# Work shared out anew between VectorE and GpSimd, and reordered edges, in a two-layer fp32 kernel on one core

## The chip, the cores and the metric

The kernel runs on one core of a Trainium2 chip. The metric is the device time in microseconds (us); here the median over runs of the whole program. The engines are TensorE (PE, with its weight loads PEld), VectorE (DVE), ScalarE (ACT), GpSimd (POOL) and SyncE (SP), which issues most DMAs.

## The reference

```python
def lora_add(base, inp, A, B):          # A, B picked per batch by itok_B_2_6
    t = jnp.einsum('bri,bni->bnr', Ab, inp)
    return base + jnp.einsum('bor,bnr->bno', Bb, t) * SCALE
gate = lora_add(jnp.einsum('bnh,fh->bnf', x, W_gate), x, A_gate, B_gate)
up = lora_add(jnp.einsum('bnh,fh->bnf', x, W_up), x, A_up, B_up)
act = jax.nn.silu(gate) * up
x = x + lora_add(jnp.einsum('bnf,hf->bnh', act, W_down), act, A_down, B_down)
...
base = jnp.einsum('bsi,oi->bso', x, weight) + bias
low = jnp.einsum('bsi,bri->bsr', x, a_sel)
x = x + base + scale[:, None, None] * jnp.einsum('bsr,bor->bso', low, b_sel)
```

x is 8 batches of 256 tokens by 1024, the hidden layer has 2752 features, all in fp32.

## The kernel before

**Numbers in two parts.** Each fp32 operand is kept as a high part (rounded to fp32r) and a low part (the rest). ACT writes the high part, then DVE or POOL subtracts it from the original and writes the low part; PE multiplies high x high, high x low and low x high. So each weight tile and each part of x takes an ACT instruction (`w_high` L1355, `x_high` L1384, `b_high` L1439) and a low one behind it (on POOL `w_low` L1784, `x_low` L1788, `ag_low` L1793; on DVE `x_low` L605, `b_low` L638). All matmuls have line L1898.

**Phase A (gate and up, to about 935 us).** The tokens are taken in two halves `h`. Each half has 22 units: 21 of 128 features (unit `u` of gate and up together) and a half tile of 64. A unit is a 2x2 block product: rows are gate (A11, A12: its tile's two chunks along the inner dimension) and up (A21, A22), columns are two groups of tokens of x (B11, B21 and B12, B22). Units 0 and 1 are plain: eight products of 12 matmuls. From the third unit on a unit takes seven products, P1 = A11 x B11, P6 = S2 x T2, P5 = S1 x T1, P7 = S3 x T3, P2 = A12 x B21, P4 = A22 x T4, P3 = S4 x B22, in that order on PE. S1 to S4 are sums of weight tiles (DVE, L530 to L540), T1 to T4 sums of x parts (DVE, `x_sum` L601); each T comes in two chunks (`kq` 0 and 1). T3 takes the place of B12. Since the T's are needed first in the third unit, they are made while units 0 and 1 run, by `first_unit(U)` and `second_unit(U)`, which exist on every engine and are each engine's hand-written order of work. The half tile (last unit of a half) has P1, P2 and a stage C = N x T2 + S x B22. ACT copies P1 to `p1buf` (`copy_p1` L1392); DVE's `add_q` (L664) adds P6 to it, which frees the bank that P7 fills; `add_v` (L670) does so ahead of P4.

**The adapters.** x times A (tiles `AG`, turned by `turn_ag`) gives t in PSUM; DVE adds its two pieces and masks each (`t_sum` L647 and L650, eight instructions), ACT makes the high part and DVE the low part (`t_low` L656, four). `Bf` is the B side of a unit (`b_low(U)`, two instructions). PE's adapters of units 0 and 1 read `Tm_g`, `Tm_u` (t) and `Bf`. Weight tiles are turned by DVE (L504), after their load by SP.

**Phase B (down projection, 935 to 1460 us).** 11 blocks, each 16 (k, pr) steps; DVE adds each result to `acc` (L923, `add_down`). `D` items are the down weights (`Wd`). The last block also sums, masks (L906) and splits the adapter's `tw_down` into `Td` (`td_low` L941) for `pr` 0 and 1, and POOL makes `X1lo` (L1842) for phase C, the second layer.

**What orders the work.** Every engine runs its own hand-written list; waits are on semaphores that count along fixed lists (`Order`: `x_sums`, `x_lo_d` for low parts on DVE, `x_lo_p` on POOL). Weight parts go through a ring of four buffers W_58 to W_61. In names of instructions X_T_51 is T2, X_T_53 is T1, X_T_54 is T3, X_T_55 is T4, X_B_49, 50 and 52 are B11, B21 and B22; xs_62 and xs_63 are buffers for T1's and T2's sums, xt_56 and xt_57 hold turned x; s_74 to s_77 are S1 to S4.

## Time and profile before

| | us |
|---|---|
| median of 3 runs (1665.5 to 1667.55) | 1667.23 |
| the profiled execution | 1668.35 |
| its span | 1666.6 |
| PE busy | 1624.7 (97%) |
| PE weight loads | 1316.6 (79%) |
| DVE | 1130.3 (68%) |
| POOL | 662.3 (40%) |
| ACT | 501.2 (30%) |

Times in the rows are in us from the span's start, durations of groups and instructions too. A row of the timeline gives start, length, engine, line, operation, tiles, count of instructions merged, and in brackets the idle time ahead of it with what ended that. Busy shares are averages over very different stretches; what counts is which wait ends last at a given place.

### The profile page before, as it was taken

The page shows a single profiled execution, that of the slowest core. Times are in us where ns is not written, and L with a number is a line of the kernel's source. Part 1 is how long each engine was busy: PE and PEld are TensorE (multiplying, and loading weights), DVE is VectorE, ACT ScalarE, POOL GpSimd, SP SyncE. Part 2 cuts the span into 40 slices and gives each one's busy share as a digit, 9 for nine tenths or more (in the row PEclk, how much of TensorE's full clock was granted, in tenths as well). Part 3 has the DMA queues.
Part 4 walks back from the last instruction along what each step waited for, and adds up shares of the span by engine and source line. Part 5 has one row for each costly group of instructions (what it writes and reads, how often), then busy time and mean ns, then how long its engine had stood idle before and what let it go on. Part 6 is the DMA issues. An engine that isn't in the chain of part 4 may idle for free.

```text
span 1666.6 us, 20956 instructions
## 1 busy us (share of the span) xinstructions
PE 1624.7 (97%) x7060; PEld 1316.6 (79%) x7060; DVE 1130.3 (68%) x1298; ACT 501.2 (30%) x833; POOL 662.3 (40%) x445
## 2 busy tenths in 40 slices
PE   5999999999999999999999999999999999999998
PEld 4778888888877788888888788888888887778886
DVE  4987777777768877777777655666665578756433
ACT  3543333333345433333334221111111122431110
POOL 4254445444453554444444443233333331541110
PEclk9999999999999999999999999999999999999999
DMA  7344434423533434344334751222222131013322
GB/s 153 82 105 105 142 93 116 143 79 86 135 86 80 105 105 143 102 107 142 83 88 131 247 147 57 53 79 80 79 53 77 61 69 28 18 29 79 79 49 55
DMA packets 218127, 156.13 MB, mean 94 GB/s; under 512 B 110692, under 2 KB 200164, under 8 KB 215268
## 3 DMA queue, kind: packets, MB, share of 16 engines
q1 hardware_dynamic: 169792, 115.05, 27.4%
q10 hardware_dynamic: 48100, 39.73, 7.5%
...
q0 software_dynamic: 128, 0.00, 0.0%
...
## 4 chain that ended last, share of the span: by engine, by line
PE 64%; DVE 1%; POOL 1%; issue 1%; ACT 0%; ACTq 0%; DVEq 0%
PE ps L1898 64%; POOL act L1824 0%; DVE acc L923 0%; POOL Wd L1832 0%; DVE tw_down L906 0%; DVE Bd L869 0%; POOL W L1784 0%; DVE tw_down L897 0%; ACT W L1355 0%; DVE TU L504 0%; DVE ct L1039 0%; DVE turned L853 0%; DVE s L530 0%; DVE co L1061 0%; DVE c21buf L683 0%
## 5 line engine op out<-in xcount | busy, mean ns | idle before, releaser
L1898 PE MATMUL ps<-act,Wd 128*128 128x512 f32 x2016 | 462.6, 390 | 4.2 <-DVE acc L923 3.1
L1898 PE MATMUL ps<-X_T,W 128*128 128x512 f32 x1944 | 460.3, 391 | 6.4 <-POOL W L1784 1.8
L1898 PEld LDWEIGHTS ps<-act,Wd 128*128 128x128 f32 x2016 | 378.5, 188 | 84.9 <-DVE acc L923 3.6
L1898 PE MATMUL ps<-X_B,W 128*128 128x512 f32 x1728 | 423.2, 395 | 22.2 <-ACT X_B L1384 13.8
L1898 PEld LDWEIGHTS ps<-X_T,W 128*128 128x128 f32 x1944 | 363.0, 188 | 91.3 <-DVE vbuf L670 7.8
L1898 PEld LDWEIGHTS ps<-X_B,W 128*128 128x128 f32 x1728 | 328.4, 191 | 95.8 <-issue 22.7
L923 DVE TENSOR_TENSOR acc<-acc,ps 128x1024 f32<-128x1024 f32 x176 | 214.4, 1220 | 183.6 <-PE ps L1898 183.1
L1784 POOL TENSOR_TENSOR W<-s,W 128x512 fp32r<-128x512 f32 x156 | 211.8, 1358 | 236.5 <-ACT W L1355 236.5
L1784 POOL TENSOR_TENSOR W<-TG,W 128x512 fp32r<-128x512 f32 x88 | 129.8, 1476 | 148.9 <-ACT W L1355 148.8
L1355 ACT ACTIVATE W<-s 128x512 fp32r<-128x512 f32 x156 | 98.7, 632 | 280.4 <-PE ps L1898 272.1
L1824 POOL TENSOR_TENSOR act<-stage,act 128x1024 fp32r<-128x1024 f32 x42 | 100.5, 2410 | 175.4 <-ACT act L1574 175.4
L1898 PE MATMUL ps<-X1hi,Wo 128*128 128x512 f32 x512 | 141.4, 390 | 0.0
L1898 PEld LDWEIGHTS ps<-X1hi,Wo 128*128 128x128 f32 x512 | 96.1, 188 | 20.6
L1574 ACT ACTIVATE act<-stage 128x1024 fp32r<-128x1024 f32 x42 | 42.6, 1050 | 186.2 <-PE ps L1898 165.6
L664 DVE TENSOR_TENSOR qbuf<-p1buf,ps 128x512 f32<-128x512 f32 x38 | 26.1, 688 | 106.1 <-PE ps L1898 105.9
L1832 POOL TENSOR_TENSOR Wd<-turned,Wd 128x512 fp32r<-128x512 f32 x44 | 55.8, 1292 | 74.0 <-ACT Wd L1608 74.0
L1355 ACT ACTIVATE W<-TG 128x512 fp32r<-128x512 f32 x88 | 55.2, 628 | 91.1 <-PE ps L1898 90.7
L1784 POOL TENSOR_TENSOR W<-TU,W 128x512 fp32r<-128x512 f32 x46 | 63.6, 1385 | 45.8 <-ACT W L1355 45.8
L1898 PE MATMUL ps<-X1lo,Wo 128*128 128x512 f32 x256 | 80.3, 390 | 0.0
L1439 ACT ACTIVATE Bf<-ts 32x256 fp32r<-32x256 f32 (+1 forms) x176 | 71.9, 409 | 1.6
L1832 POOL TENSOR_TENSOR Wo<-turned,Wo 128x512 fp32r<-128x512 f32 x16 | 21.7, 1381 | 126.7 <-ACT Wo L1608 126.7
L686 DVE TENSOR_TENSOR c21buf<-c21buf,s1buf 128x512 f32<-128x512 f32 x38 | 68.7, 1808 | 1.3
...
## 6 DMA issues: line engine op xcount, KB each, us to landing
...
```

Source lines behind the costliest of these rows:

```text
L664: V.tensor_tensor(qbuf[:, :], p1buf[:, :], bank(U % 2, "b"), ALU.add).then_inc(q_done, 1)
L686: V.tensor_tensor(c21buf[:, :], c21buf[:, :], s1buf[:, :], ALU.mult).then_inc(act1_done, 1)
L923: V.tensor_tensor(acc[pr][:, k, :], acc[pr][:, k, :], src[:, :], ALU.add).then_inc(b_added.up(s), 1)
L1355: A.activation(hi, src, ACT.Copy).then_inc(w_hi, 1)
L1439: last = A.activation(home, src, ACT.Copy)
L1574: A.activation(acts[t % 3][:, 0, cols], stage[t % 2][:, cols], ACT.Copy).then_inc(act_hi.up((t, pr)), 1)
L1784: G.tensor_tensor(low, src, hi.bitcast(F32), ALU.subtract).then_inc(w_lo, 1)
L1824: G.tensor_tensor(acts[t % 3][:, 1, cols], stage[t % 2][:, cols], acts[t % 3][:, 0, cols].bitcast(F32), ALU.subtract).then_inc(act_lo.up(( ...
L1832: last = G.tensor_tensor(low, src, hi.bitcast(F32), ALU.subtract)
L1898: return nc.tensor.matmul(dst, stationary, moving, start=start, stop=stop, skip_group_check=True)
```

## The change

1. T2's sum always goes to xs_63 (before, its two chunks used both buffers). The order of sums becomes T1, T2, T1, T4, T2, T3, T3, T4; T4's first sum is made ahead of `t_sum` in the first unit.
2. The low parts of T2 (both chunks) and of T1's second go from DVE to POOL.
3. In the second unit DVE turns the third unit's tiles and makes S1, S2 ahead of T3, T4 and of the plain units' activations; ACT and POOL follow.
4. Half tile: PE does N x T2 between P1 and P2; in half 0's DVE makes B21's low part before it turns Ag. ACT and POOL write N ahead of A12.
5. The first down product waits for its low weight part four matmuls later.
6. Last block: masks leave `add_down` and become `td_mask`, pair 0 directly ahead of its low parts, pair 1 after the add (5, 0), low parts of pair 1 after (6, 0); ACT makes `Td`'s high part of pair 1 one X1hi later.
7. Eight DMAs of Ag(0, 0) are issued by ACT instead of SP.

```diff
@@ -138,7 +138,7 @@
                 return xs[0][:, :, :]
             if name == "T2":
-                return xs[1 - kq][:, :, :]
+                return xs[1][:, :, :]
...
@@ -203,7 +203,7 @@
             if u == FULL:
-                return ["P1", "P2", "C"]
+                return ["P1", "N", "P2", "C"]
...
@@ -301,16 +301,16 @@
                          [i for i in RAW_ORDER if i[0] in "xy" and i[:2] != ("x", 0)])
         x_sums = Order("x_sums", [(h, n, kq) for h in range(HALVES) for n, kq in (
-            ("T1", 0), ("T2", 0), ("T1", 1), ("T2", 1), ("T3", 0), ("T3", 1), ("T4", 0), ("T4", 1))])
...
         x_lo_d = Order("x_lo_d", [(h, n, kq) for h in range(HALVES) for n, kq in (
             *((("B11", 0), ("B21", 0), ("B12", 0)) if h == 0 else (("B12", 0), ("B11", 0), ("B21", 0))),
-            ("B11", 1), ("B12", 1), ("T1", 0), ("T2", 0), ("T1", 1), ("T2", 1), ("T4", 1), ("T3", 1))])
+            ("B11", 1), ("B12", 1), ("T1", 0), ("T3", 1), ("T4", 1))])
         x_lo_p = Order("x_lo_p", [(h, n, kq) for h in range(HALVES) for n, kq in (
-            ("B22", 0), ("B21", 1), ("B22", 1), ("T4", 0), ("T3", 0))])
+            ("B22", 0), ("B21", 1), ("B22", 1), ("T2", 0), ("T1", 1), ("T2", 1), ("T3", 0), ("T4", 0))])
...
@@ -586,7 +586,8 @@
                     summed("T1", kq)
                     if kq == 1:
-                        wait_x_low(eng, h, "T1", 1)
+                        wait_x_low(eng, h, "T2", 0)
+                        summed("T4", 0)
...
@@ -749,6 +750,7 @@
                 b_low(U)
+                x_sum(h, "T4", 0)
                 for p in range(2):
...
@@ -756,27 +758,24 @@
                 b_low(U + 1)
-                x_low(h, "T2", 0)
-                x_low(h, "T1", 1)
                 x_sum(h, "T2", 1)
+
+            def second_unit(U):
+                h = U // UNITS
+                turn_tile(("G", U + 1))
+                turn_tile(("U", U + 1))
+                sums(U + 1, (1, 2))
                 x_sum(h, "T3", 0)
                 x_sum(h, "T3", 1)
-                x_low(h, "T2", 1)
-                x_sum(h, "T4", 0)
-                x_sum(h, "T4", 1)
-
-            def second_unit(U):
-                h = U // UNITS
+                sums(U + 1, (3, 4))
                 plain_act1(U - 1)
                 plain_act2(U - 1)
-                turn_tile(("G", U + 1))
-                turn_tile(("U", U + 1))
-                x_low(h, "T4", 1)
-                sums(U + 1, (1, 2, 3, 4))
+                x_sum(h, "T4", 1)
                 plain_act1(U)
                 turn_b(("b", h, 1))
                 x_low(h, "T3", 1)
                 b_low(U + 1)
+                x_low(h, "T4", 1)
                 plain_act2(U)
             def unit(U):
...
@@ -820,9 +819,9 @@
                     x_low(1, "B12", 0)
                     x_low(1, "B11", 0)
+                    x_low(1, "B21", 0)
                     turn_ag(("Ag", 1, 0))
                     half_tile_first(U)
-                    x_low(1, "B21", 0)
                 else:
...
@@ -893,18 +892,10 @@
-                        n = 3 * pr + 2 * p
                         V.tensor_tensor(one, one, part[0:Q, :], ALU.add).then_inc(td_summed, 1)
-                        eng.wait_ge(td_summed, n + 1)
-                        if p == 0:
-                            V.tensor_tensor(one, one, part[Q:2 * Q, :], ALU.add).then_inc(td_summed, 1)
-                            eng.wait_ge(td_summed, n + 2)
-                        else:
-                            V.tensor_tensor(one, one, part[Q:2 * Q, :], ALU.add).then_inc(b_added.up(s), 1)
-                            eng.wait_ge(b_added.sem, b_added.after(s))
-                        one = one.rearrange("p (b t) -> p b t", b=2)
-                        V.tensor_tensor(one, one, pick_half[:, 0:2].unsqueeze(2).to_broadcast([Q, 2, NS]), ALU.mult
-                                        ).then_inc(td_masked, 1)
+                        eng.wait_ge(td_summed, 3 * pr + 2 * p + 1)
+                        V.tensor_tensor(one, one, part[Q:2 * Q, :], ALU.add
+                                        ).then_inc(*((td_summed, 1) if p == 0 else (b_added.up(s), 1)))
                 elif k == "t":
                     cols = slice(pr * T, (pr + 1) * T)
...
@@ -922,6 +913,14 @@
+
+            def td_mask(pr):
+                eng.wait_ge(td_summed, 3 * pr + 2)
+                eng.wait_ge(b_added.sem, b_added.after((BLOCKS - 1, "t", pr)))
+                for p in range(2):
+                    one = tw_down[:, pr * T:][:, p * TT:(p + 1) * TT].rearrange("p (b t) -> p b t", b=2)
+                    V.tensor_tensor(one, one, pick_half[:, 0:2].unsqueeze(2).to_broadcast([Q, 2, NS]), ALU.mult
+                                    ).then_inc(td_masked, 1)
...
@@ -971,11 +970,14 @@
+                        td_mask(0)
                         td_low(0, 0)
                         td_low(0, 1)
                     elif (k, pr) == (0, 0):
                         last_low(1)
                     elif (k, pr) == (5, 0):
+                        td_mask(1)
+                    elif (k, pr) == (6, 0):
                         td_low(1, 0)
                         td_low(1, 1)
...
@@ -1483,24 +1487,24 @@
                 b_high(U + 1)
-                x_high(h, "T2", 1)
             def second_unit(U):
                 h = U // UNITS
                 silu_first(U - 1)
                 silu_plain(U - 1)
+                x_high(h, "T2", 1)
+                w_high(U + 1, "A11")
+                w_high(U + 1, "S2")
+                silu_first(U)
+                store_act(U - 1)
+                w_high(U + 1, "S1")
+                x_high(h, "T3", 0)
+                x_high(h, "T3", 1)
+                w_high(U + 1, "S3")
                 x_high(h, "T4", 0)
                 x_high(h, "T4", 1)
-                silu_first(U)
-                store_act(U - 1)
-                w_high(U + 1, "A11")
-                w_high(U + 1, "S2")
+                b_high(U + 1)
                 silu_plain(U)
-                x_high(h, "T3", 0)
-                w_high(U + 1, "S1")
-                x_high(h, "T3", 1)
-                w_high(U + 1, "S3")
-                b_high(U + 1)
             def unit(U):
                 h, u = divmod(U, UNITS)
...
@@ -1683,6 +1687,7 @@
             w_high(0, "A21")
             w_high(0, "A22")
+            ag_rows(eng, raw[n % RAW], raw_full[n % RAW], 1, first_rows)
             x_high(0, "B12", 0)
...
@@ -1808,15 +1813,18 @@
                 for item in ("A11", "A12", "A21", "A22"):
                     w_low(U + 1, item)
+                x_low(h, "T2", 0)
+                x_low(h, "T1", 1)
             def second_unit(U):
                 h = U // UNITS
-                x_low(h, "T4", 0)
+                x_low(h, "T2", 1)
                 w_low(U + 1, "A11")
                 w_low(U + 1, "S2")
+                w_low(U + 1, "S1")
                 x_low(h, "T3", 0)
-                w_low(U + 1, "S1")
                 w_low(U + 1, "S3")
+                x_low(h, "T4", 0)
             def act_low(t, pr):
                 cols = slice(pr * T, (pr + 1) * T)
...
@@ -2079,13 +2085,13 @@
+                free_c(U)
+                wait_w_low(eng, U, "N")
+                up(U, "N", product(U, "N", "T2", c))
                 eng.wait_ge(p1_done, seven_half(U))
                 stage_p(U, "P2", a, start=False)
                 adapter(U, 0, 0, a)
                 up(U, "P2", adapter(U, 1, 0, a))
-                free_c(U)
-                wait_w_low(eng, U, "N")
-                product(U, "N", "T2", c)
                 wait_w_low(eng, U, "S")
...
@@ -2121,6 +2127,9 @@
+                    if s == (0, 0, 0) and c == 0 and wl == 1:
+                        for e in range(2):
+                            eng.wait_ge(it_lo.sem, it_lo.after(("D", 0, e)))
                     for p in range(2):
...
@@ -2161,7 +2170,11 @@
-                    eng.wait_ge(it_lo.sem, it_lo.after(("D", bb, e)))
+                    if bb == 0:
+
+                        eng.wait_ge(it_hi.sem, it_hi.after((("D", 0, e), 1)))
+                    else:
...
```

The order of the instructions on three engines:

POOL around its first units, before: behind A22's low part of unit 1 (W_61 from TU) come T4 and the third unit's A11.

```order
L1784 TENSOR_TENSOR W_60<-TU,W_60 128x512
L1784 TENSOR_TENSOR W_61<-TU,W_61 128x512
L1788 TENSOR_TENSOR X_T_55<-xt_56,X_T_55 128x1024
L1784 TENSOR_TENSOR W_58<-TG,W_58 128x512
L1784 TENSOR_TENSOR W_59<-s_75,W_59 128x512
L1788 TENSOR_TENSOR X_T_54<-xt_56,X_T_54 128x1024
L1784 TENSOR_TENSOR W_60<-s_74,W_60 128x512
L1784 TENSOR_TENSOR W_61<-s_76,W_61 128x512
```

And after: three low parts of T2 and T1 come first.

```order
L1789 TENSOR_TENSOR W_60<-TU,W_60 128x512
L1789 TENSOR_TENSOR W_61<-TU,W_61 128x512
L1793 TENSOR_TENSOR X_T_51<-xs_63,X_T_51 128x1024
L1793 TENSOR_TENSOR X_T_53<-xs_62,X_T_53 128x1024
L1793 TENSOR_TENSOR X_T_51<-xs_63,X_T_51 128x1024
L1789 TENSOR_TENSOR W_58<-TG,W_58 128x512
L1789 TENSOR_TENSOR W_59<-s_75,W_59 128x512
L1789 TENSOR_TENSOR W_60<-s_74,W_60 128x512
L1793 TENSOR_TENSOR X_T_54<-xt_56,X_T_54 128x1024
L1789 TENSOR_TENSOR W_61<-s_76,W_61 128x512
L1793 TENSOR_TENSOR X_T_55<-xt_56,X_T_55 128x1024
```

T4 went from the front of that stretch to its end, T2, T1, T2 are new in it, and S1 (from s_74) stands ahead of T3.

DVE behind b_low(1), before (L601 are T sums, L708 and L714 `plain_act1` and `plain_act2`):

```order
L601 TENSOR_TENSOR xs_62<-xt_57,xs_62 128x1024
L601 TENSOR_TENSOR xt_56<-xt_56 128x2x512
L601 TENSOR_TENSOR xt_56<-xt_57 128x2x512
L605 TENSOR_TENSOR X_T_51<-xs_62,X_T_51 128x1024
L601 TENSOR_TENSOR xt_56<-xt_56,xs_63 128x2x512
L601 TENSOR_TENSOR xt_56<-xt_57,xs_62 128x2x512
L708 TENSOR_TENSOR c21buf<-s1buf,ps 128x512
L714 TENSOR_TENSOR vbuf<-qbuf,ps 128x512
L504 STREAM_TRANSPOSE TG<-raw_67 128x1024
L504 STREAM_TRANSPOSE TU<-raw_68 128x1024
L605 TENSOR_TENSOR X_T_55<-xt_56,X_T_55 128x1024
L530 TENSOR_TENSOR s_74<-TU 128x512
```

And after:

```order
L602 TENSOR_TENSOR xs_63<-xt_57,xs_62 128x1024
L504 STREAM_TRANSPOSE TG<-raw_67 128x1024
L504 STREAM_TRANSPOSE TU<-raw_68 128x1024
L530 TENSOR_TENSOR s_74<-TU 128x512
L535 TENSOR_TENSOR s_75<-s_74,TG 128x512
L602 TENSOR_TENSOR xt_56<-xt_56 128x2x512
L602 TENSOR_TENSOR xt_56<-xt_57 128x2x512
L537 TENSOR_TENSOR s_76<-TG,TU 128x512
L540 TENSOR_TENSOR s_77<-TG,s_75 128x512
L709 TENSOR_TENSOR c21buf<-s1buf,ps 128x512
L715 TENSOR_TENSOR vbuf<-qbuf,ps 128x512
L602 TENSOR_TENSOR xt_56<-xt_57,xs_63 128x2x512
```

The turns (L504) and S1 and S2 moved ahead of T3's sums and of the activations; the low part of T2 (into X_T_51) is gone from DVE, T4's (X_T_55) comes later, behind the next b_low, and of T4's sums only one is left here.

PE in the half tile of half 0, before (W_60 is A12, W_61 is N):

```order
L1898 MATMUL ps<-X_B_49,W_59 128x512 x12
L1898 MATMUL ps<-X_B_50,W_60 128x512 x12
L1898 MATMUL ps<-Tm_g,Bf_88 128x512
L1898 MATMUL ps<-Tm_u,Bf_88 128x512
L1898 MATMUL ps<-X_T_51,W_61 128x512 x12
```

And after (W_60 is N, W_61 is A12):

```order
L1904 MATMUL ps<-X_B_49,W_59 128x512 x12
L1904 MATMUL ps<-X_T_51,W_60 128x512 x12
L1904 MATMUL ps<-X_B_50,W_61 128x512 x12
L1904 MATMUL ps<-Tm_g,Bf_88 128x512
L1904 MATMUL ps<-Tm_u,Bf_88 128x512
```

The product with T2 moved from behind P2 and its adapters to between P1 and P2.

## Rows read from the trace of the kernel before

**Rows 1.** The page: PE's busy time, share of the span, instructions.

```profile
PE 1624.7 (97%) x7060; PEld 1316.6 (79%) x7060; DVE 1130.3 (68%) x1298; ACT 501.2 (30%) x833; POOL 662.3 (40%) x445
```

**Rows 2.** Waits of PE: line <- releaser, us in total, times, longest.

```profile
PE ps L1898 <- ACT X_B L1384: 13.8, 1, 13.8
...
PE ps L1898 <- DVE acc L923: 3.1, 1, 3.1
PE ps L1898 <- POOL AG L1793: 2.5, 1, 2.5
PE ps L1898 <- DVE X_B L605: 1.9, 1, 1.9
PE ps L1898 <- POOL W L1784: 1.8, 1, 1.8
...
PE ps L1898 <- POOL Wd L1832: 1.1, 1, 1.1
```

**Rows 3.** Windows: us, busy time and instructions of five engines, PEclk, DMA.

```profile
81.00:85.00 4.00, 4.00 (x13) 3.09 (x12) 3.52 (x6) 3.23 (x5) 2.52 (x2) 0.57 0.41 93
100.00:150.00 50.00, 50.00 (x219) 40.79 (x218) 37.02 (x44) 18.20 (x33) 23.04 (x17) 1.00 0.37 94
...
544.00:548.00 4.00, 2.17 (x11) 1.49 (x10) 3.92 (x4) 1.97 (x4) 4.00 (x3) 1.00 0.43 128
```

**Rows 4.** Timeline of SP, half 0 front.

```profile
24.29 3.84 SPq L454 DMA_DIRECT2D raw<-in_L_cond_A_up_dram  x8
```

**Rows 5.** Timeline of ACT, half 0 front.

```profile
21.69 1.06 ACT L1384 ACTIVATE X_T<-xt 128x1024 fp32r<-128x1024 f32 x1 [5.42 <-DVE xt L570]
```

**Rows 6.** Timeline of DVE, half 0, 50 to 66 us.

```profile
51.14 2.31 DVE L601 TENSOR_TENSOR xs<-xt 128x1024 f32<-128x1024 f32 x1
53.48 1.83 DVE L638 TENSOR_TENSOR Bf<-ts,Bf 32x256 fp32r<-32x256 f32 x2
...
64.07 0.85 DVE L638 TENSOR_TENSOR Bf<-ts,Bf 32x256 fp32r<-32x256 f32 x2 [0.55 <-ACT Bf L1439]
64.95 1.23 DVE L605 TENSOR_TENSOR X_T<-xs,X_T 128x1024 fp32r<-128x1024 f32 x1
```

**Rows 7.** Timeline of PE, half 0, units 1 and 2.

```profile
64.97 0.50 PE L1898 MATMUL ps<-Tm_g,Bf 96*128 96x512 f32 x1
...
80.55 4.58 PE L1898 MATMUL ps<-X_B,W 128*128 128x512 f32 x12 [3.48 <-issue]
...
91.88 3.02 PE L1898 MATMUL ps<-X_T,W 128*128 128x512 f32 x12 [0.18 <-DVE qbuf L664]
...
98.74 1.45 PE L1898 MATMUL ps<-X_T,W 128*128 128x512 f32 x5 [0.66 <-DVE vbuf L670]
```

**Rows 8.** Timeline of POOL, half 0, 50 to 80 us.

```profile
51.07 3.53 POOL L1784 TENSOR_TENSOR W<-TU,W 128x512 fp32r<-128x512 f32 x2 [3.52 <-ACT W L1355]
75.73 2.39 POOL L1788 TENSOR_TENSOR X_T<-xt,X_T 128x1024 fp32r<-128x1024 f32 x1 [21.13 <-ACT X_T L1384]
```

**Rows 9.** Timeline of PE, half tile of half 0 and start of half 1.

```profile
470.98 3.02 PE L1898 MATMUL ps<-X_B,W 128*128 128x512 f32 x12 [0.69 <-ACT p1buf L1392]
...
483.68 5.95 PE L1898 MATMUL ps<-X_B,W 128*128 128x512 f32 x18 [1.86 <-DVE X_B L605]
```

**Rows 10.** Timeline of DVE, half 1.

```profile
504.00 1.25 DVE L504 STREAM_TRANSPOSE TU<-raw 128x1024 f32<-128x1024 f32 x1 [1.60 <-DMA raw<-in_L_cond_W_up_dram]
...
521.27 0.85 DVE L638 TENSOR_TENSOR Bf<-ts,Bf 32x256 fp32r<-32x256 f32 x2 [0.62 <-ACT Bf L1439]
...
548.45 0.69 DVE L664 TENSOR_TENSOR qbuf<-p1buf,ps 128x512 f32<-128x512 f32 x1
```

**Rows 11.** Timeline of DVE, last block.

```profile
1431.86 2.60 DVE L906 TENSOR_TENSOR tw_down<-tw_down,pick_half 32x512 f32<-32x512 f32 x1
...
1435.91 1.32 DVE L906 TENSOR_TENSOR tw_down<-tw_down,pick_half 32x512 f32<-32x512 f32 x1
...
1445.97 1.22 DVE L923 TENSOR_TENSOR acc<-acc,ps 128x1024 f32<-128x1024 f32 x1 [1.69 <-PE ps L1898]
```

29 lines of the change are left out of this document (15 added, 14 removed).

## The prediction

> **What bounds the kernel now.** I read the page first: TensorE (PE) is busy 1624.7 of 1666.6 us [rows 1]. So the change is worth what it does to PE's 42 us of idle time, and to the clock behind an idle stretch. The list of PE's waits comes next [rows 2]: 13.8 us are the start, which no edit touches; the rest are single gaps, each at one place. Then the granted clock by windows [rows 3]: over 50 undisturbed microseconds it is 1.00 (2.4 GHz) and PE runs 219 matmuls, 0.228 us each, so 2.7 us for a product of 12. In the 4 us behind the 3.48 us gap [rows 7] the mean is 0.57, which is 3.4 us at the lower level, 1.2 GHz, and costs half of that, **1.7 us**. I found the same behind the gaps of 2.5, 1.9 and 3.1 us; behind the one of 1.8, for a weight's low part [rows 2], which ends at 546.3, the clock stayed at 1.00 [rows 3]. A gap of over 2 us is thus priced with 1.7 on top, one of 1.8 with nothing or 1.7. Last I read when each engine does what PE waits for, at the four places that the change touches.
>
> **Front, half 0.** Eight DMA issues of 3.84 us leave SP's queue [rows 4]; they go to ACT's, where 5.42 us of idle time stand ahead of 21.69 us [rows 5], so they cost nothing there. What SP fed comes 3.84 us earlier: the 2.5 us wait [rows 2] for Ag's low part goes, and its clock. That alone were 3.84 us, if all later work had followed.
>
> **T chain, half 0.** It does not follow. Before, VectorE (DVE) does b_low(0) from 53.48, the eight steps of t_sum, four of t_low, then b_low(1) from 64.07 to 64.92 [rows 6]; PE takes the adapters that read them at 64.97 [rows 7]. There is no slack: PE leaves when DVE is done. The change puts T4's first sum on DVE ahead of t_sum, some 1.2 us by the like instruction at 64.95 [rows 6], and two low parts on GpSimd (POOL) directly behind A22's low part. POOL had nothing to do from 54.60 to 75.73, 21.13 us [rows 8], so POOL has the time. But do the two engines run side by side? A DVE sum of two SBUF tiles took 2.31 us at 51.14 next to POOL's low parts, and two b_low took 1.83 [rows 6], against 1.23 for such a sum without POOL at 64.95 and 0.85 for two b_low at 64.07 [rows 6]. They took turns. A POOL low part of 128x1024 lasts 2.39 [rows 8]. So the cost has the ends 1.2 (only T4's sum) and 1.2 + 2 x 2.39 = 6.0 (both low parts in full). I take **5.5**: t_sum reads PSUM and may run its first 0.68 us next to POOL, its mask, which reads SBUF twice, may not. Half 0: 5.5 - 3.84 = **+1.7** at the adapters. What DVE loses here it gets back later (two low parts, 2.4 us, behind b_low(1)).
> The Trainium skill, page "SBUF — State Buffer", section "Who interferes with whom", says that a DVE instruction with two SBUF inputs contends with a GpSimd instruction that reads SBUF, and that the one which issued first holds the shared ports to its end; by it the sum takes the 5.5, and without it 1.2, which would turn the total below from +2.1 to -6.5. By that rule these low parts are in the wrong place, and [rows 6] agree with it.
>
> **Third unit.** It is the first with seven products. Before, PE waits 3.48 us for its P1 (A11's low part sat on POOL behind T4's), with 1.7 of clock, and 0.18 ahead of P7 [rows 7]. The new order of DVE turns G and U first, then S1 and S2, and POOL's queue has A11 and S2 behind one low part only, so P1, P6 and P5 should go without a wait. P7 however needs the q add, which still stands behind plain_act2, both b_low and now T4,1's low part too. Before, q comes 26.9 us behind b_low(1) (64.92 to the start of P7 at 91.88 [rows 7]; in half 1 from 522.12 to the add's end at 549.14 [rows 10], 27.0). For the new order I add DVE's list: T2 sum 1.23, two turns 2.45, four S sums and two T3 sums 5.2 with about 5 us of turns taken with POOL, two plain_act 1.4; then silu_first(U) on ACT, 0.6, which has to await plain_act1, and behind it ten ACT instructions (S1, T3 twice, S3, T4 twice, b_high four times), 7.2 us with 1.06 for a part of X [rows 5], an estimated 0.63 for a weight part of half that size and 0.42 for each of the four small ones (half of DVE's pair [rows 6]), then b_low 0.85, T4,1's low part 1.2, act2 and q 1.4: 3.7 + 10.2 + 1.4 + 0.6 + 7.2 + 3.4 = **26.5** (ends 23 and 29, by how many turns are taken). So P7 starts 0.5 earlier against b_low(1), and PE, having had no earlier wait, stands still some 6 us ahead of it (its work from the adapters to P1 is 80.55 - 3.48 - 64.97 = 12.1, and three products are 8.2, so it is there at 20.3): one gap in place of several, and behind it a slow clock, so that P7, P2 and two adapters take 6.2 + 1.7 = 7.9 until P4 instead of 6.86 (91.88 to 98.74 [rows 7]): +1.0. Half 0 in sum: 1.7 - 0.5 + 1.0 = **+2.2**.
>
> **Half tile and half 1.** N x T2 before P2 covers the copy of P1 (0.69 at 470.98; I take 0.87 with what stands around it), B21's low part ahead of Ag's turns removes the 1.86 us wait and its clock, 1.7 [rows 9]. PE is then 4.6 us earlier at Ag. DVE is not: U's tile is turned at 504.00 after a wait of 1.60 for its load [rows 10], and SP issues that when the slots ahead of it are free; only the 1.86 carries over. In this half too the adapters wait for DVE: b_low(1) ends at 522.12 [rows 10]. So the chain: -1.85 + 5.5 - 0.5, and +1.0 behind P7: **+4.2**. Both low-part edits fall on the same chain, and PE's 4.6 us are spent in waiting.
>
> **D(0).** PE waits 1.06 us for POOL's last Wd low part [rows 2]. Now it may run four matmuls first, 4 x 0.228: **-0.9**. POOL's own chain is not moved.
>
> **Last block.** Between two accumulations DVE did four sums and two masks; the masks took 2.60 and 1.32 (taking turns with X1lo on POOL) [rows 11], and PE stood 3.1 us for the accumulation behind them [rows 2], with 1.7 of clock [rows 3]. Masks moved to behind block (5,0): 4.8 us go. Given back: there the two masks and one X1lo in their way are 1.36 + 2.4 = 3.8 us, the slack of DVE per block is about 1.7 (idle 1.69 before the add at 1445.97 [rows 11]), so DVE is 2.1 late, td_low comes in the next block and may meet POOL once more, and the first block of pair 1 needs its Td. I take 1.4 given back, between 0 and 3.1: **-3.4**, ends -4.8 and -1.7.
>
> **Costed at nothing:** T2 in its own buffer (removes an order between sum and low part, DVE was not waiting for it), the split of add_down, ACT's order in the half tile, x1_high moved ahead of td_high(1).
>
> **Sum.** 2.2 + 4.2 - 0.9 - 3.4 = **+2.1** on the profiled execution's 1668.35, which lies 1.1 above the median 1667.23. Forecast for the median: **1669.3 us**. A measurement of this kernel can tell some 0.2% (3.3 us) from no change, so this counts as the same (bound 1670.6).
>
> **Rivals.**
> *Faster: the low parts do not stretch the chain* (POOL's X_T lows come when DVE is in turns or PSUM sums; U's turn took 1.25 [rows 10], no more than any other). For it: only b_low, T4's sum and masks are exposed, and T1,1's high part may be late enough. Against it: 2.31 and 1.83 in [rows 6]. It gives back 4.3 per half: 2.1 - 8.6 = -6.5, **1660.7**. Chance 0.17.
> *Faster: the third unit does what its order is made for.* If q comes 23 us behind b_low(1), P7 waits 2.5 us less in each half and the clock may stay: 2.1 - 7 = -5, **1662.3**. For it: P1, P6 and P5 surely lose their waits. Against: the silu of unit U now waits behind four sums. Chance 0.13.
> *Slower: td's low part becomes what the last block waits for, and T3's and T4's low parts are late.* Td(1)'s masks and low parts each meet an X1lo of 2.4 on POOL; if the first two-input operation is behind a POOL instruction in each of the two blocks, DVE is 3.8 + 3.7 - 3.4 = 4.1 late, and it decides from the point where that exceeds one bank's 2.8 us: a gap with a slow clock comes back, -3.4 becomes 0. With q at 29 us in one half (+2.5) the sum is 2.1 + 3.4 + 2.5 = +8, at the first alone +5.5: **1672.7** for that one mechanism. Against it: 1.7 us slack in each block. Chance 0.22.
> *The earlier front changes nothing,* since SP's next loads wait for slots that DVE frees: +3.84, then 1673. It is in the 0.22.
>
> **Chances.** My forecast with its own spread, 1666 to 1672, has 0.48: of it 0.34 within 0.2%, 0.12 slower, 0.02 faster. With the rivals: faster 0.32, same 0.34, slower 0.34. The range must leave out no more than the outer halves of both ends: **1659 to 1675**.
>
> **What would show it.** Right: the wait for Ag's low part (2.5) is gone from PE's list and PE waits 5 to 6 us ahead of the adapters of units 0 and 1 in both halves; POOL's X_T lows lie between two b_low of over 1.3 us; PE waits some 6 us for q at P7 with clock below 0.6 behind; the last block shows no wait above 1.5. Wrong: b_low(0) takes 0.85 and t_sum starts at 51.5 to 53 us; P7 within 24 us of b_low(1); a wait for Td in the last block of over 3 us.

## The result, and the profile after

| | before | after |
|---|---|---|
| median | 1665.35 us (6 runs, 1663.57 to 1667.55) | 1672.07 us (6 runs, 1670.06 to 1674.03) |
| ratio | | 1.0039, interval 1.0029 to 1.0049 |
| profiled execution | 1668.35 us, span 1666.6 | 1672.3 us, span 1670.6 |
| mean granted clock | 0.995 | 0.991 |
| time lost at the lower clock | 9.5 us | 11.2 us |

The change makes the kernel slower by 0.39%. The forecast was 1669.3, within 0.2% of before; its range, 1659 to 1675, holds the result. Between the two profiled executions the difference is +4.0 us where I had +2.1.

The last line of the table is counted from the trace, over the stretches where consecutive matmuls of 512 columns start over 0.35 us apart without a wait: the time above 0.227 us each. Left out are three starts in each half of after, 0.60 us apart, at the adapters of units 0 and 1: there PE follows DVE's four `t_low`, which start 0.60 us apart too. So only 1.7 of the 4.0 us are clock; the rest is waiting.

The page of after, PE's and the other engines' share:

```profile
PE 1627.8 (97%) x7060; PEld 1319.0 (79%) x7060; DVE 1138.7 (68%) x1292; ACT 501.8 (30%) x833; POOL 675.2 (40%) x451
```

The list of PE's waits (line <- releaser, us in total, times, longest):

```profile
PE ps L1904 <- ACT X_B L1388: 12.8, 1, 12.8
PE ps L1904 <- DVE qbuf L665: 9.5, 2, 5.4
PE ps L1904 <- DVE Tm_g L657: 6.6, 2, 3.5
...
PE ps L1904 <- POOL Wd L1840: 1.3, 1, 1.3
PE ps L1904 <- DVE Td L940: 1.1, 1, 1.1
```

Against [rows 2], PE no longer waits for Ag's low part, for B21's low part, for a weight's low part or for `acc`; it waits twice for the masked T (`Tm_g`), 6.6 us in all, and twice for the q add, 9.5.

DVE's timeline in half 0 (start, us, engine line op, tiles; in brackets the idle time before it), which answers to [rows 6]:

```profile
48.78 3.95 DVE L639 TENSOR_TENSOR Bf<-ts,Bf 32x256 fp32r<-32x256 f32 x2
52.77 3.30 DVE L602 TENSOR_TENSOR xt<-xt,xs 128x1024 f32<-128x1024 f32 x1
55.99 0.67 DVE L648 TENSOR_TENSOR tw<-tw,ps 32x512 f32<-32x512 f32 x1
...
64.70 0.85 DVE L639 TENSOR_TENSOR Bf<-ts,Bf 32x256 fp32r<-32x256 f32 x2 [0.54 <-ACT Bf L1443]
```

And POOL's there, which answers to [rows 8]:

```profile
46.21 3.69 POOL L1789 TENSOR_TENSOR W<-TU,W 128x512 fp32r<-128x512 f32 x2 [3.30 <-ACT W L1359]
49.87 5.12 POOL L1793 TENSOR_TENSOR X_T<-xs,X_T 128x1024 fp32r<-128x1024 f32 x2
```

b_low(0), two instructions that take 0.85 us when POOL rests, took 3.95, and T4's sum 3.30 in place of 1.22. From b_low(0)'s start to `t_sum` it is 7.21 us, before 1.86 (53.48 to 55.34). DVE came to b_low(0) 4.7 us earlier than before and began b_low(1) 0.63 later.

PE in half 0, which answers to [rows 7]:

```profile
62.50 0.76 PE L1904 MATMUL ps<-Tm_g,Bf 96*128 96x512 f32 x1 [3.48 <-DVE Tm_g L657]
...
65.60 0.79 PE L1904 MATMUL ps<-Tm_g,Bf 96*128 96x512 f32 x1 [0.53 <-DVE Bf L639]
...
79.20 2.90 PE L1904 MATMUL ps<-X_B,W 128*128 128x512 f32 x12
81.95 5.60 PE L1904 MATMUL ps<-X_T,W 128*128 128x512 f32 x24
92.97 4.61 PE L1904 MATMUL ps<-X_T,W 128*128 128x512 f32 x12 [5.43 <-DVE qbuf L665]
...
100.63 2.93 PE L1904 MATMUL ps<-X_T,W 128*128 128x512 f32 x12
```

P1, P6 and P5 (36 matmuls from 79.20) run without a wait, and then all that was saved is waited for at once ahead of P7. Behind that wait PE did 12 matmuls in 4.61 us instead of 2.9. Windows behind the two waits for q (us, busy time and instructions of five engines, clock, DMA):

```profile
93.00:97.00 4.00, 4.00 (x11) 3.19 (x12) 3.05 (x4) 0.75 (x2) 2.53 (x2) 0.57 0.61 186
554.00:560.00 6.00, 5.32 (x13) 4.16 (x14) 5.01 (x6) 1.15 (x2) 2.53 (x2) 0.50 0.44 138
```

The start of each matmul in after, less that of the same one in before, gives the balance by place. The first starts 0.92 earlier, an early start of the profiled execution: `last_only`, below, whose edit is all in the last block, starts 0.78 earlier too.

| stretch | measured | forecast |
|---|---|---|
| half 0, to P4 of the third unit | +2.80 | +2.2 |
| rest of half 0 (waits of 0.26 and 0.21 at 161.5 and 242.4, less those of before) | +0.26 | 0 |
| half tile and half 1, to P4 of its third unit | +5.30 | +4.2 |
| rest of half 1 | +0.12 | 0 |
| second half tile | -1.13 | 0 |
| D(0) | +0.65 | -0.9 |
| last block | -3.09 | -3.4 |
| sum, from the first matmul (the span's +4.0 has the 0.92 in it) | +4.91 | +2.1 |

Inside the first row PE gains 4.2 by Ag and keeps it to the adapters; inside the third row it gains 4.7 by Ag. Both gains end at the next wait for DVE.

### The profile page after: what moved, and what is told of

Read it like the earlier page. It is cut to its first block, busy times and chain, and to the rows that moved or that the text cites. A ratio compares the mean times of both kernels' runs of the same rounds, so it can differ in the third digit from the quotient of the medians.

```text
span 1670.6 us, 20955 instructions
## 1 busy us (share of the span) xinstructions
PE 1627.8 (97%) x7060; PEld 1319.0 (79%) x7060; DVE 1138.7 (68%) x1292; ACT 501.8 (30%) x833; POOL 675.2 (40%) x451
## 4 chain that ended last, share of the span: by engine, by line
PE 64%; DVE 1%; POOL 1%; issue 0%; DMA 0%; ACT 0%; SPq 0%; DVEq 0%
PE ps L1904 64%; DVE tw_down L922 0%; POOL act L1832 0%; POOL Wd L1840 0%; DVE acc L914 0%; DMA raw<-in_x_dram 0%; POOL W L1789 0%; DVE Bd L868 0%; DVE tw_down L897 0%; DVE tw_down L895 0%; ACT W L1359 0%; DVE ct L1041 0%; DVE turned L852 0%; SPq L1171 0%; DVE X_T L606 0%
## 5 line engine op out<-in xcount | busy, mean ns | idle before, releaser
L1904 PE MATMUL ps<-X_T,W 128*128 128x512 f32 x1944 | 466.7, 395 | 11.8 <-DVE qbuf L665 9.5
L1904 PEld LDWEIGHTS ps<-X_T,W 128*128 128x128 f32 x1944 | 369.0, 191 | 96.8 <-DVE qbuf L665 10.3
L1904 PE MATMUL ps<-X_B,W 128*128 128x512 f32 x1728 | 418.9, 392 | 13.7 <-ACT X_B L1388 12.8
L1904 PEld LDWEIGHTS ps<-X1hi,Wo 128*128 128x128 f32 x512 | 96.1, 188 | 20.6
L1904 PE MATMUL ps<-X1lo,Wo 128*128 128x512 f32 x256 | 80.3, 390 | 0.0
L639 DVE TENSOR_TENSOR Bf<-ts,Bf 32x256 fp32r<-32x256 f32 (+1 forms) x88 | 72.1, 819 | 5.2 <-ACT Bf L1443 3.3
```

The source lines that it names most:

```text
L639: last = V.tensor_tensor(dst, src, hi.bitcast(F32), ALU.subtract)
L1904: return nc.tensor.matmul(dst, stationary, moving, start=start, stop=stop, skip_group_check=True)
```

## The experiments

The diffs of `edges` and of its parts are against before, those of the others against after, except where the text names another. Each was timed against new runs of before, whose medians were 1665.41 (for `lows_back`, `t4_late`, `unit2_back` and `edges`), 1665.41 (for `lows_hidden`, `act_first`, `q_first` and `all_three`) and 1665.71 (for the rest), with 21 to 31 runs each.

**Two theories on the T chain: ports or T4's sum.** `lows_back` gives the two low parts back to DVE, behind b_low(1), and keeps everything else.

```diff
                 b_low(U + 1)
+                x_low(h, "T2", 0)
+                x_low(h, "T1", 1)
                 x_sum(h, "T2", 1)
...
-                x_low(h, "T2", 0)
-                x_low(h, "T1", 1)
```

> The changed kernel with the low parts of T2,0 and T1,1 back on VectorE behind b_low(1); T4's first sum stays ahead of t_sum. Ports theory: b_low(0) falls from 3.95 to about 1.8 us and T4's sum from 3.30 to 1.2, so t_sum starts 4 to 5 us earlier in both halves; VectorE has 2.4 us more to do before the q add, so P7 comes 2 to 2.5 us earlier per half: about 1667.5 us, some 2 above the kernel before. Rival (VectorE is late for another reason, the start of b_low is bound by loads): t_sum stays at about 56 us, and the 2.4 us come on top: 1677.

Measured: 1665.45 us, ratio 0.9998 (0.9989 to 1.0007); that is 6.6 us below after, and 2 below what the ports theory gave. DVE's timeline:

```profile
48.72 1.83 DVE L639 TENSOR_TENSOR Bf<-ts,Bf 32x256 fp32r<-32x256 f32 x2
50.58 1.22 DVE L602 TENSOR_TENSOR xt<-xt,xs 128x1024 f32<-128x1024 f32 x1
51.73 0.67 DVE L648 TENSOR_TENSOR tw<-tw,ps 32x512 f32<-32x512 f32 x1
...
75.25 0.69 DVE L709 TENSOR_TENSOR c21buf<-s1buf,ps 128x512 f32<-128x512 f32 x1
```

The same b_low(0), at the same time (48.72), takes 1.83, the sum 1.22, and `t_sum` starts 4.3 us earlier. Nothing but the two low parts was moved, so they are what held DVE. But PE does not get all of it:

```profile
76.04 3.00 PE L1904 MATMUL ps<-X_B,W 128*128 128x512 f32 x12 [2.54 <-issue]
...
90.13 3.35 PE L1904 MATMUL ps<-X_T,W 128*128 128x512 f32 x7 [5.66 <-DVE qbuf L665]
```

PE waits 2.54 ahead of P1, which starts 0.10 us after the end of `plain_act1` (75.25 to 75.94), for whose count PE waits there (`free_a`). In the new order of the third unit that instruction stands behind T3's sums, S3 and S4. So the new order, which I had costed only through q, has a second price, which in after the late adapters covered.

`t4_late` keeps the low parts on POOL and moves T4's first sum to behind b_low(1).

```diff
                 b_low(U)
-                x_sum(h, "T4", 0)
...
                 b_low(U + 1)
+                x_sum(h, "T4", 0)
```

> The changed kernel with T4's first sum behind b_low(1), low parts stay on GpSimd. Ports theory: GpSimd's second low part now meets b_low and t_sum's first mask, so the chain gains only the sum's own 1.2 us plus at most 1 us, and the sum costs 1.2 us behind the chain: 1670.5 to 1672, within 0.1% of the changed kernel. Rival (the 3.30 us sum is the whole of the stretch): adapters 3.3 us earlier in both halves, 1668.

Measured: 1671.2 us, ratio 1.0034 (1.0022 to 1.0046), as the ports theory had it; it is 0.9 less than after, which the two intervals don't separate. This trace also shows which of DVE's instructions the low parts hold (POOL is at them from 49.72 to 54.84):

```profile
52.62 0.67 DVE L648 TENSOR_TENSOR tw<-tw,ps 32x512 f32<-32x512 f32 x1
53.32 2.06 DVE L651 TENSOR_TENSOR tw<-tw,pick_half 32x512 f32<-32x512 f32 x1
```

The sum that reads PSUM takes its usual 0.67; the mask behind it, of the same size but with both inputs in SBUF, takes 2.06 instead of 0.68.

**Is the third unit's new order any good?** `unit2_back` keeps all of the change but gives DVE, ACT and POOL their order of before in the second unit (shown for DVE; on ACT and POOL T4's first parts go ahead of T3's again).

```diff
                 x_sum(h, "T2", 1)
+                x_sum(h, "T3", 0)
+                x_sum(h, "T3", 1)
+                x_sum(h, "T4", 1)
...
+                plain_act1(U - 1)
+                plain_act2(U - 1)
                 turn_tile(("G", U + 1))
                 turn_tile(("U", U + 1))
-                sums(U + 1, (1, 2))
-                x_sum(h, "T3", 0)
-                x_sum(h, "T3", 1)
-                sums(U + 1, (3, 4))
-                plain_act1(U - 1)
-                plain_act2(U - 1)
-                x_sum(h, "T4", 1)
+                x_low(h, "T4", 1)
+                sums(U + 1, (1, 2, 3, 4))
...
                 b_low(U + 1)
-                x_low(h, "T4", 1)
```

> The changed kernel with the order before in the second unit (activations, then turns; T4 ahead of T3) on all three engines. If the q add is bound by the same list of work in any order, PE waits again ahead of P1 (about 3.5 us) and no more for 5.4 at P7; the total stays within 2 us of the changed kernel, 1670 to 1674. Rival 1 (the new order is what helps): 5 us slower per half, 1682. Rival 2 (the new order is what costs): 1666.

Measured: 1665.31 us, ratio 0.9999 (0.999 to 1.0008), 6.8 us below after. I had expected the total to stay, and was wrong: the second rival (the new order is what costs) gave 1666. PE's timeline:

```profile
64.85 0.80 PE L1903 MATMUL ps<-Tm_g,Bf 96*128 96x512 f32 x1 [0.52 <-DVE Bf L639]
...
86.08 3.00 PE L1903 MATMUL ps<-X_T,W 128*128 128x512 f32 x12 [1.60 <-issue]
89.25 3.01 PE L1903 MATMUL ps<-X_T,W 128*128 128x512 f32 x12 [0.17 <-DVE qbuf L665]
```

P7 starts 24.4 us behind the adapters (64.85 to 89.25); in after it is 27.4 (65.60 to 92.97), before 26.9. With POOL's low parts on the chain and the old order, PE loses 1.60 and 0.17 in the third unit and has no stretch of slow clock there. In half 1 no wait of that unit is above 1.44 us. So either of two parts of the change, undone alone, gives back the whole 6.7 us. DVE's timeline shows where the 3.0 us between 27.4 and 24.4 come from:

```profile
75.34 1.21 DVE L606 TENSOR_TENSOR X_T<-xt,X_T 128x1024 fp32r<-128x1024 f32 x1
...
84.89 2.81 DVE L639 TENSOR_TENSOR Bf<-ts,Bf 32x256 fp32r<-32x256 f32 x2
```

The third unit's b_low starts 20.0 us behind the adapters (in after 20.6) and takes 2.81 (in after 4.05), and T4,1's low part is done long before it (75.34), where in after it stands between b_low and q and takes 1.1 more. These are 0.6, 1.2 and 1.1 us.

`lows_hidden` keeps the low parts on POOL, but behind b_low(1), so that they fall into DVE's turns, which read one tile.

```diff
                     w_low(U + 1, item)
+                eng.wait_ge(bf_lo, U + 2)
                 x_low(h, "T2", 0)
                 x_low(h, "T1", 1)
...
                 turn_tile(("U", U + 1))
+                x_sum(h, "T2", 1)
```

> The changed kernel with one wait more: GpSimd starts the low parts of T2,0 and T1,1 only when b_low(1) is done, and VectorE makes T2,1's sum behind the two turns instead of ahead of them. No instruction changes its engine. Ports theory: b_low(0) 1.8 and T4's sum 1.2 us, t_sum 4 us earlier against U's turn in both halves, the turns beside GpSimd's low parts stay at 1.25 us; the q add about 4 us earlier: 1664. Rival (an instruction costs VectorE the same wherever GpSimd's falls, the stretch only moves behind b_low(1)): 1672.

Measured: 1669.19 us, ratio 1.0024 (1.0015 to 1.0034), between the theory's 1664 and the rival's 1672. POOL's two low parts:

```profile
61.31 4.76 POOL L1793 TENSOR_TENSOR X_T<-xs,X_T 128x1024 fp32r<-128x1024 f32 x2 [11.53 <-DVE Bf L639]
```

and DVE beside them:

```profile
61.26 1.25 DVE L504 STREAM_TRANSPOSE TG<-raw 128x1024 f32<-128x1024 f32 x1
62.43 1.20 DVE L504 STREAM_TRANSPOSE TU<-raw 128x1024 f32<-128x1024 f32 x1
63.80 3.35 DVE L602 TENSOR_TENSOR xs<-xt,xs 128x1024 f32<-128x1024 f32 x1 [0.17 <-issue]
...
68.90 5.65 DVE L602 TENSOR_TENSOR xt<-xt 128x1024 f32<-128x1024 f32 x2
```

The turns lose nothing beside POOL (1.25 and 1.20); the first sum behind them loses 2.1, and T3's sums 3.2 (2.45 alone, by twice the 1.22 of one sum) since POOL is now later there too. DVE was freed by 4.3 us at `t_sum` and q came only 1.0 earlier. The contention was moved, not removed.

**Activations ahead of the sums.** `act_first` is `lows_back` with `plain_act1` and `plain_act2` ahead of T3's sums and T4's first sum behind b_low(1) (of its diff, the activations).

```diff
                 sums(U + 1, (1, 2))
+                plain_act1(U - 1)
+                plain_act2(U - 1)
                 x_sum(h, "T3", 0)
                 x_sum(h, "T3", 1)
                 sums(U + 1, (3, 4))
-                plain_act1(U - 1)
-                plain_act2(U - 1)
```

> lows_back with T4's first sum behind b_low(1) and plain_act1 and plain_act2 of unit 0 ahead of T3's sums, S3 and S4. In lows_back PE waited 2.5 us ahead of P1, and the trace has plain_act1 ending 0.1 us before P1 starts; ACT's silu of unit 1, S1, T3, T4 and b_high all stand behind it. Theory (plain_act1's place is what the new order costs): no wait ahead of P1, the q add 2 to 4 us earlier in both halves, 1659 to 1662. Rival (VectorE's sum of work sets q in any order): q within 0.5 us, 1664 to 1666.

Measured: 1664.91 us, ratio 0.9995 (0.9985 to 1.0004): the rival was right. PE:

```profile
75.15 5.60 PE L1904 MATMUL ps<-X_T,W 128*128 128x512 f32 x24
89.86 5.49 PE L1904 MATMUL ps<-X_T,W 128*128 128x512 f32 x12 [9.11 <-DVE qbuf L665]
```

The wait ahead of P1 is gone (the 36 matmuls of P1, P6 and P5 end at 80.75), and P7 starts where it did (89.86 against 90.13): the time went into one wait of 9.11 us. Removing a wait that ends ahead of another, on a chain that does not run through PE, moves it. What sets the time is q.

`q_first` goes for q itself: b_low of the third unit and T4,1's low part go behind the q add on DVE, and ACT does the silu that `plain_act2` reads, and the copy of P1, ahead of T4's high parts; v is added ahead of the next sums (diff against `act_first`).

```diff
                 x_low(h, "T3", 1)
-                b_low(U + 1)
-                x_low(h, "T4", 1)
                 plain_act2(U)
...
                 add_q(U)
+                if u == PLAIN:
+                    b_low(U)
+                    x_low(h, "T4", 1)
...
                 w_high(U + 1, "S3")
+                silu_plain(U)
+                copy_p1(U + 1)
                 x_high(h, "T4", 0)
```

> act_first, and the third unit's b_low and T4,1's low part behind the q add, silu_plain and copy_p1 ahead of T4's high parts on ACT, v ahead of the fourth unit's sums. Theory: q 20 to 23 us behind b_low(1) instead of 27 to 29, the wait ahead of P7 under 2 us and no slow clock behind it: 1651 to 1656. Rival (what is moved behind q makes v late and PE waits ahead of P4 instead): P4 no earlier than in act_first, about 1660.

Measured: 1654.28 us, ratio 0.9935 (0.9919 to 0.9952), the fastest of all and faster than both kernels. PE's and then DVE's timeline:

```profile
84.49 4.39 PE L1909 MATMUL ps<-X_T,W 128*128 128x512 f32 x12 [4.37 <-DVE qbuf L665]
```

```profile
81.86 1.20 DVE L606 TENSOR_TENSOR X_T<-xt,X_T 128x1024 fp32r<-128x1024 f32 x1
...
83.75 0.69 DVE L665 TENSOR_TENSOR qbuf<-p1buf,ps 128x512 f32<-128x512 f32 x1
```

q starts at 83.75, in `act_first` at 89.12. b_low and T4,1's low part, which there took 1.89 and 2.23 us in q's way, behind an idle 1.03 us, now come behind it. The run moved ACT's work and v at the same time, so the time shows what these edits give together, and the rows show that b_low and the low part make up most of it. The gap ahead of P7 is still 4.37, where I had expected under 2, so there is more to be had.

`all_three` adds to `q_first` the placement of `lows_hidden`: the two low parts on POOL, beside turns and activations; T4's first and T2's second sum stand behind these, S1 and S2 behind the sums, and A11 ahead of T2's second part on ACT and POOL (diff against `q_first`).

```diff
-                x_low(h, "T2", 0)
-                x_low(h, "T1", 1)
...
+                eng.wait_ge(bf_lo, U + 2)
+                x_low(h, "T2", 0)
+                x_low(h, "T1", 1)
```

> q_first with the low parts of T2,0 and T1,1 on GpSimd as in the change, but started behind b_low(1) only, where VectorE has two turns and two activations from PSUM to do. Ports theory: those two low parts (2.4 us of VectorE) are then free, 1 to 2 us faster than q_first: 1650 to 1655. Rival: T2,1's sum waits for GpSimd's T2,0 and the list is no shorter, same as q_first within 1 us.

Measured: 1660.62 us, ratio 0.9968 (0.9956 to 0.9981), a miss: 6.3 us above `q_first`. DVE:

```profile
63.67 2.30 DVE L602 TENSOR_TENSOR xt<-xt,xs 128x1024 f32<-128x1024 f32 x1
66.11 2.09 DVE L602 TENSOR_TENSOR xs<-xt,xs 128x1024 f32<-128x1024 f32 x1
...
69.52 5.67 DVE L602 TENSOR_TENSOR xt<-xt 128x1024 f32<-128x1024 f32 x2
...
76.82 2.89 DVE L540 TENSOR_TENSOR s<-TG,s 128x512 f32<-128x512 f32 x1
```

In `q_first` DVE does both low parts itself in 2.36 us and the T3 sums in 4.18. Here it is spared the 2.36 and pays 1.1 and 0.9 on two sums, 1.5 on T3's and 2.2 on S4; q starts at 85.29, 1.5 later, and the slow clock behind it cost 3.0 us in half 0 where `q_first` lost 1.5.

**The edges.** `edges` is before with the front, half tile, D(0) and last block of the change, and nothing of its T chain or its third unit; of its diff, which is that of the four parts, the lines of D(0), which no other run has alone:

```diff
+                    if s == (0, 0, 0) and c == 0 and wl == 1:
+                        for e in range(2):
+                            eng.wait_ge(it_lo.sem, it_lo.after(("D", 0, e)))
```

> The kernel before with the edges alone: half tile, D(0), last block and Ag's loads; T sums, low parts and second unit as before. Theory: front 4.2 us, half tile 2 to 5 (the chain of half 1 may hide the rest), D(0) 0.5, last block 3.1 are all kept: 10 to 13 us faster than before, ratio 0.992 to 0.994. Rival (the chain is bound by loads that SP issues, the front's gain is lost at the adapters anyway): 4 to 6 us faster, ratio 0.997.

Measured: 1657.4 us, ratio 0.9949 (0.9936 to 0.9963), 8.0 us faster than before, between the 10 to 13 that I had expected and the rival's 4 to 6. The edges are good; what stands beside them in the change costs 14.7 us (1672.07 - 1657.4). By the same count the new order alone costs 8.0 (`lows_back` less `edges`) and the low parts alone 7.9 (`unit2_back` less `edges`). T4's early sum is in both counts, and even so they add up to 15.9: the two costs are nearly additive. Then three of the edges alone. `last_only`:

```diff
                     if (k, pr) == ("t", 0):
+                        td_mask(0)
                         td_low(0, 0)
...
                     elif (k, pr) == (5, 0):
+                        td_mask(1)
+                    elif (k, pr) == (6, 0):
                         td_low(1, 0)
```

> The kernel before with the last block's edit alone. By the changed kernel's trace the matmuls behind it lose 3.1 to 3.2 us of delay there (wait of 3.1 and its slow clock gone, 1.1 us waiting for Td given back): 3.2 us faster, ratio 0.9981. Rival (the slow clock behind the wait is not there in most executions): 1.5 to 2 us faster.

Measured: 1663.18 us, ratio 0.9985 (0.9976 to 0.9994): -2.5, between the theory's 3.2 and the rival's 1.5 to 2; in the trace the last block is 3.1 shorter.

`front_only`:

```diff
             w_high(0, "A22")
+            ag_rows(eng, raw[n % RAW], raw_full[n % RAW], 1, first_rows)
             x_high(0, "B12", 0)
```

> The kernel before with Ag's eight loads on ACT's queue alone. By the traces 4.2 us earlier at the first Ag matmuls, and in the kernel with all edges and no T edits this stays to the end of half 0: 4 us faster, ratio 0.9976. Rival (slots of loads give it back at the adapters): under 1.5 us.

Measured: 1661.6 us, ratio 0.9976 (0.9967 to 0.9986): -4.1, and it is kept to the end.

`half_only`:

```diff
-                return ["P1", "P2", "C"]
+                return ["P1", "N", "P2", "C"]
...
                     x_low(1, "B11", 0)
+                    x_low(1, "B21", 0)
                     turn_ag(("Ag", 1, 0))
                     half_tile_first(U)
-                    x_low(1, "B21", 0)
```

> The kernel before with the half tile's edits alone. PE 5.0 us earlier at half 1's first product; behind the adapters of half 1, where VectorE's chain sets the time, 2 us of it left, and 1.1 at the second half tile: 3.0 to 3.3 us faster, ratio 0.998. Rival (all 5 us carried): 6 us faster, ratio 0.9964.

Measured: 1665.39 us, ratio 0.9997 (0.9988 to 1.0006), a miss. By the half tile's edit PE is 4.7 us earlier at Ag, 3.0 of it is left behind the third unit, and 1.15 comes at the second half tile. Then, at the first down product:

```profile
934.62 10.73 PE L1896 MATMUL ps<-act,Wd 128*128 128x512 f32 x39 [2.18 <-POOL Wd L1832]
```

with this window behind it:

```profile
933.00:939.00 6.00, 4.38 (x12) 3.51 (x13) 5.31 (x12) 1.88 (x3) 4.63 (x4) 0.72 0.99 378
```

PE waits 2.18 for POOL's low part of Wd, 1.1 more than before, and the clock falls, for about 1.6 us. The two together give back 2.8. That leaves 1.4 us in this trace, and the medians show 0.3; the rest is not explained. In `edges`, where the product may begin four matmuls earlier, PE meets the same point so:

```profile
929.77 1.09 PE L1902 MATMUL ps<-act,Wd 128*128 128x512 f32 x4
932.19 18.19 PE L1902 MATMUL ps<-act,Wd 128*128 128x512 f32 x79 [1.33 <-POOL Wd L1838]
```

1.33, and no slow stretch. That no slow stretch came there I put down to the D(0) edit, and with it that the parts (4.1 + 2.5 + 0.3 = 6.9) give less than `edges` (8.0); D(0) alone was not run, so this is argued from two traces, not shown.

**One more way to q.** `edges_q` is `edges` with the order of DVE made for q: G turned ahead of the activations, T4's sums behind U's turn, b_low behind q, and A11 ahead of T4 on ACT and POOL (diff against `edges`).

```diff
                 add_q(U)
+                if u == PLAIN:
+                    b_low(U)
...
+                turn_tile(("G", U + 1))
                 plain_act1(U - 1)
                 plain_act2(U - 1)
-                turn_tile(("G", U + 1))
                 turn_tile(("U", U + 1))
+                x_sum(h, "T4", 0)
+                x_sum(h, "T4", 1)
                 x_low(h, "T4", 1)
```

> The kernel edges, and for the third unit: b_low behind the q add, G turned ahead of the plain units' activations, T4's sums behind U's turn, A11 ahead of T4 on ACT and GpSimd; T1 and T2 low parts all on VectorE. If what counts is the place of single steps (A11's low part for P1, b_low for q) and not which engine has T's low parts: the wait ahead of P1 falls from 3.4 to about 1, q comes 3 us earlier: 1650 to 1653, as fast as q_first (1654.3) or faster. Rival (the low parts on VectorE hold q back): 1656 to 1658, no gain on edges.

Measured: 1662.34 us, ratio 0.9983 (0.9973 to 0.9992), a miss: 5 us above `edges`. P1 (72.28) has no wait, P6 has:

```profile
81.94 10.37 PE L1903 MATMUL ps<-X_T,W 128*128 128x512 f32 x33 [6.76 <-DVE c21buf L708]
```

The trace names `c21buf`, which had been written by 81.31; what ended at 81.84 is the low part of S2, on POOL, and its cause is on DVE:

```profile
80.31 1.53 POOL L1791 TENSOR_TENSOR W<-s,W 128x512 fp32r<-128x512 f32 x1 [3.28 <-ACT W L1361]
```

```profile
75.58 2.54 DVE L605 TENSOR_TENSOR X_T<-xt,X_T 128x1024 fp32r<-128x1024 f32 x1 [2.12 <-ACT X_T L1390]
...
78.82 0.69 DVE L535 TENSOR_TENSOR s<-s,TG 128x512 f32<-128x512 f32 x1
```

S2's sum (78.82) stood behind T4,1's low part, and that behind ACT's high part, for which ACT in turn waited:

```profile
73.54 2.01 ACT L1390 ACTIVATE X_T<-xt 128x1024 fp32r<-128x1024 f32 x2 [3.38 <-DVE xt L601]
```

It waited for T4's second sum, which ends at 73.45 here and at 69.84 in `edges`: my edit had put T4's sums behind U's turn on DVE. I left S1 and S2 where they were and moved what fed the instruction ahead of them.

## Why the prediction was right or wrong

**Front: right.** -4.2 for -3.84 in the trace, -4.1 alone in `front_only`. And DVE's chain came forward with it: in `lows_back`, `edges` and after, DVE starts b_low(0) at 48.7 to 48.8 (before 53.48).

**T chain: right, in size and cause.** 5.5 was taken between 1.2 and 6.0. Measured from b_low(0) to `t_sum` it is 5.35 in half 0 and 5.45 in half 1 (510.78 to 518.10, before 510.61 to 512.48). `lows_back` shows the low parts as the cause: without them 4.2 of it go and 1.2 stay, T4's sum. The Trainium skill ("SBUF — State Buffer", "Who interferes with whom") states that a DVE instruction with two SBUF inputs contends with a GpSimd instruction that reads SBUF. This trace agrees: such instructions on DVE took 3.95 and 3.30 beside POOL's 5.12. The wait ahead of the adapters was 3.5 and 3.1 where the text says 5 to 6, with a slow clock behind it (1.7 and 2.7 us) that I had not forecast; it cost nothing, since the wait for q behind it took it up.

**Third unit: the step that failed.** "P7 starts 0.5 earlier against b_low(1)": it is 27.4 behind in half 0 (before 26.9) and 27.0 in half 1 (as before), where 26.5 was taken. The parts of that sum: to T4's sum 15.3 was taken and 14.8 measured (65.55 to 80.3); ACT's part took 5.9 (to 86.24) where I added 7.8; and from b_low to q's end it was 6.7 for 3.4. (T4's second sum, 1.2 us, is in the measured 14.8, and I had left it out of the 15.3.) In the last part "then b_low 0.85" is the error, as b_low meets POOL's low parts of T4 (86.24 to 88.61) and of the third unit's A12 (88.57 to 90.01):

```profile
86.24 4.05 DVE L639 TENSOR_TENSOR Bf<-ts,Bf 32x256 fp32r<-32x256 f32 x2 [1.11 <-ACT Bf L1443]
```

It took 4.05, in q's way, about as b_low(0) had; in half 1 it took 4.08. I had applied the rule of the T chain to the first b_low and not to the third. The trace of before could have told me: there the third took 2.82 already, beside POOL's low parts.

```profile
87.51 2.82 DVE L638 TENSOR_TENSOR Bf<-ts,Bf 32x256 fp32r<-32x256 f32 x2
```
P1, P6 and P5 did lose their waits, and the one for q is 5.4 and 4.1 ("some 6"). From P7 to P4 the text adds 1.0 for the clock; it was +0.8 in half 0 (7.66 for 6.86) and **+1.95** in half 1 (8.81 for 6.86), where the clock is 0.50 over all of 554 to 560.

What I did not see at all is that this order is worse in itself. The list of DVE lost two low parts (2.4 us), and with the old order P7 does come 24.4 behind (`unit2_back`, 2.5 less than before); the new order gives 3.0 back, 1.2 of it by b_low and 1.1 by T4,1's low part behind it. The rival "does what its order is made for" asked for 23, and the old order came nearer to that than the new one. And `plain_act1`, for me one more entry of DVE's list, also lets P1 begin; the late adapters hid that, and `lows_back` brought it out as 2.54 us.

**Half tile: right at its place,** -4.7 for -4.6. "Only the 1.86 carries over" holds by its size: DVE starts b_low(0) of half 1 0.17 later than before, where PE had come into the half tile 2.14 later, so 2.0 carry. But "in this half too the adapters wait for DVE" was read wrongly: before, b_low(1) ended at 522.12 and PE took it at 524.85, 2.7 us later. That did no harm to the sum because P7 starts when q is done in either kernel. The stretch came to +5.3 for +4.2, by the clock behind P7 (1.95 for 1.0) and by P7 itself, which came no earlier against b_low(1). Not forecast: the copy of P1 is passed in the second half tile too, -1.13.

**D(0): wrong in size.** -0.9 was forecast, +0.65 measured: PE came 1.13 earlier to a POOL that did not follow, and waits 1.33 behind its four matmuls. With the second half tile it is -0.5.

**Last block: right.** -3.1 for -3.4. The masks met X1lo once more (5.21 us for two) and PE waits 1.15 for the result, then no slow stretch:

```profile
1441.74 5.21 DVE L922 TENSOR_TENSOR tw_down<-tw_down,pick_half 32x512 f32<-32x512 f32 x2
```

```profile
1448.95 1.01 PE L1904 MATMUL ps<-Td,Bd 96*128 96x512 f32 x2 [1.15 <-DVE Td L940]
```

The slower rival, by which DVE would be over 2.8 us late there and a slow clock would follow, is refuted, though its number (1672.7) is the nearest to the result.

**Before's own number.** I priced everything on a profiled execution of 1668.35 and took it as 1.1 above the median. The 74 later runs of before have medians of 1665.4 to 1665.7, so it was 3.0 above; after's profiled execution is 0.2 above its median. The 1667.23 to which I added the 2.1 was 1.8 too high as well: from 1665.4 I would have forecast 1667.5, 4.6 below the result. That 1669.3 came within 2.8 us of it is partly luck. Trace against trace the change is +4.0, median against median +6.7. The 2.7 between them is not explained: one profiled execution per kernel can't tell whether before's stretches of slow clock (9.5 us in this one) are fewer in its other executions.

**The sum.** Counted from the first matmul it was 2.8 too low: D(0) 1.55, half 1 1.1, half 0 0.6, small waits behind them 0.4, last block 0.3, less 1.1 of the second half tile. In the medians the change is +6.7, three times the 2.1. The forecast itself called for no change within 0.2%, a case with a chance of 0.34; measured is 0.39% slower, and slower had 0.34 too.
